# Routing phase: the root chain of a later round's norm on VectorE is woven between the ranking and the one-hot rows of this round

## What is computed

```python
h = _layernorm(x, axis=-1) * (1 + cb) + sb
X = h.reshape(-1, D)                       # 8192 tokens, D = 128
scores = sigmoid(X @ gate_w.T)             # E = 32 experts
_, idx = top_k(scores + bias, K)           # K = 4
w = take_along_axis(scores, idx, axis=-1)
w = w / clip(sum(w, axis=-1), 1e-12)
eid = idx.reshape(-1)
onehot = (eid[:, None] == arange(E)[None, :])
pos = take_along_axis(cumsum(onehot, axis=0) - 1, eid[:, None], axis=1)[:, 0]
valid = pos < C                            # C = 128 places per expert
...
xe = zeros((E, C, D)).at[eid, posc].add(where(valid[:, None], Xrep, 0))
```

## Time and profile before

| | us |
|---|---|
| median of 3 runs (lowest, highest) | 2204.21 (2203.22, 2204.34) |
| the profiled execution's own time | 2207.98 |
| its span, first to last instruction | 2206.2 |
| mean granted TensorE clock over the span | 0.869 of full |
| routing: DVE's first transpose of variances starts | 645.30 |
| routing: the last product `unit` (round 7) starts | 777.48 |
| routing: DVE's last instruction starts | 822.18 |

### The profile page before, as it was taken

How to read it: one execution, slowest core, us unless ns; L and a number is a source line. 1 busy time by engine, 2 the same in 40 slices (tenths; PEclk the granted TensorE clock), 3 DMA queues, 4 the chain that set the end, 5 groups by cost and what they waited for, 6 DMA issues and landing times. The chain is left out here.

```text
span 2206.2 us, 44205 instructions
## 1 busy us (share of the span) xinstructions
PE 1723.8 (78%) x13783; PEld 1360.8 (62%) x13783; DVE 1614.0 (73%) x4636; ACT 1338.3 (61%) x3234; POOL 1164.1 (53%) x1240
## 2 busy tenths in 40 slices
PE   5589999999956749569985777777777642999994
PEld 5478888888733434246653555555556532999993
DVE  7689999999948863369877999999655442555554
ACT  4468777777736882157764888887344331555551
POOL 3178777777710007722324888888525454444440
PEclk8699999999977658879987999999766555999997
DMA  3000000000040102341100000000311012222218
GB/s 114 14 2 2 2 2 2 2 2 2 2 182 31 41 30 47 39 133 58 48 1 1 1 1 1 1 1 1 155 34 35 32 40 62 68 66 65 65 50 233
DMA packets 103365, 92.10 MB, mean 42 GB/s; under 512 B 11696, under 2 KB 93616, under 8 KB 102432
## 3 DMA queue, kind: packets, MB, share of 16 engines
q1 hardware_dynamic: 80128, 62.84, 9.3%
q0 software_dynamic: 14560, 22.24, 3.8%
q10 hardware_dynamic: 8448, 4.20, 0.6%
HBM read 46.32 MB, written 42.91 MB: 40 GB/s over the span
## 5 line engine op out<-in xcount | busy, mean ns | idle before, releaser
L2253 POOL TENSOR_TENSOR delta_A<-delta_A,delta_sW 128x256 f32<-128x256 f32 x256 | 193.9, 758 | 79.5 <-ACT delta_sW L2100 53.5
L2023 PE MATMUL delta_u<-delta_m,tables_sb 128*128 128x256 f32 x512 | 166.7, 407 | 82.3 <-DVE delta_m L2173 82.3
L2873 POOL DMA_INDIRECT choice_rows<-ffn_y,ffn_xg x135 | 129.8, 962 | 169.9 <-DVE ffn_y L2980 164.7
L645 ACT ACTIVATE attn_p_att<-attn_score,attn_mx 128x224 f32<-128x224 f32 (+7 forms) x512 | 146.1, 397 | 107.2 <-DVE attn_mx L735 107.2
L630 ACT ACTIVATE attn_p_geo<-attn_kp_wide,attn_geo_cols 128x32 f32<-128x32 f32 (+6 forms) x448 | 179.5, 503 | 0.0
L2100 ACT ACTIVATE delta_sW<-delta_W,tables_sb 128x256 f32<-128x256 f32 x256 | 126.7, 506 | 80.5 <-DVE delta_W L2195 76.7
L573 PE MATMUL attn_score<-attn_k,attn_q_diag 128*128 128x64 f32 (+5 forms) x1024 | 175.4, 314 | 0.0
L2023 PEld LDWEIGHTS delta_u<-delta_m,tables_sb 128*128 128x128 f32 x512 | 87.3, 190 | 133.1 <-DVE delta_m L2173 126.3
L2019 PE MATMUL delta_u<-delta_v_own,tables_sb 128*128 128x256 f32 x512 | 154.1, 383 | 8.7 <-DVE xnT L2160 8.7
L587 PE MATMUL attn_out<-attn_turned,attn_v_diag 64*64 64x256 f32 (+7 forms) x4096 | 142.4, 288 | 14.6 <-DVE attn_turned L756 12.0
L2830 POOL DMA_INDIRECT rows<-mix_rows,mix_slot x128 | 124.3, 971 | 55.6 <-issue 51.5
(11 more groups left out here) (399 smaller groups left out, 4938.4 us busy)
## 6 DMA issues: line engine op xcount, KB each, us to landing
ffn_xg<-rows SPq DMA_DIRECT2D x135, 66.0 KB
acc<-route_zero SPq DMA_DIRECT2D x10, 832.0 KB
comb_rows<-choice_rows SPq DMA_DIRECT2D x32, 256.0 KB
rows<-route_rows SPq DMA_DIRECT2D x8, 640.0 KB, 3.4
load_rows<-in_x SPq DMA_DIRECT2D x16, 256.0 KB, 4.3
bT<-acc SPq DMA_DIRECT2D x16, 256.0 KB, 4.1
qT<-acc SPq DMA_DIRECT2D x16, 256.0 KB, 4.9
x_kept<-xT SPq DMA_DIRECT2D x16, 256.0 KB, 2.1
```

The costliest lines, as they stand in the source:

```text
L645: last = nc.scalar.activation(p_att[:, gr, PAIR_OFF[n]:PAIR_OFF[n] + SLOT * (n + 1)], score[at][:, c:c + SLOT * (n + 1)], ACT.Exp, bias=mx ...
L2023: nc.tensor.matmul(corrections(h, pp % 2), g.t("same_head"), m1[:, h].rearrange("p t d b -> p (t d b)"), start=False, stop=True).then_inc( ...
L2253: nc.gpsimd.tensor_tensor(A[:, t % 8], A[:, (t - 1) % 8], sW[:, t % RING], ALU.add).then_inc(k.A, 1)
L2873: nc.gpsimd.indirect_dma_start(g.choice_rows, bass.IndirectOffsetOnAxis(xg[:, n % RING, D:D + 1].bitcast(U32), 0), y[:, n % RING, :], None ...
```

## The change

In rounds 0 to 5, DVE no longer runs `norm(i + 2)` and then `rank(i)`. A new function `rank_beside_norm(i)` first places round i (`place`, `base`), and then issues the steps of the norm of round m = i + 2 alternately with the remaining steps of the ranking: the transpose of the variances, `own`, the add of epsilon, `slot`, the guess, the first one-hot row, and then each of the seven root steps followed by one more row. `spread_norm(m)`, the second transpose and the product `unit`, comes last. `rank` is split into `rank`, `own_places`, `own_slots` and `slot_row`. Each one-hot row now adds one to `by_slot_rest`, so its readers wait for 8 per round instead of 1. Rounds 6 and 7 and the norms of rounds 0 and 1 keep their order. Nothing is computed differently.

```diff
             def add_slots(i):
                 pe.wait_ge(c.by_slot, i + 1)
-                pe.wait_ge(c.by_slot_rest, i + 1)
+                pe.wait_ge(c.by_slot_rest, (CHOICES - BY_ACT) * (i + 1))
...
                 refine_roots(nc, dve, root_y[:, :], root_t[:, :], root_v[:, :], c.newton, ROOT * i)
+                spread_norm(i)
+
+            def spread_norm(i):
                 dve.wait_ge(c.newton, ROOT * (i + 1))
...
                 nc.vector.tensor_tensor(base[:, :], base[:, :], counts[:, SIDE * E0:WIDTH], ALU.add).then_inc(c.counted, 1)
+
+            def own_places(i):
+                dve.wait_ge(c.placed, i + 1)
                 nc.vector.tensor_tensor(own[:, :, :, :], onehots(i), place[:, :, None, :].to_broadcast([128, SIDE, K0, E0]),
                                         ALU.mult).then_inc(c.owned, 1)
+
+            def own_slots(i):
                 dve.wait_ge(c.owned, i + 1)
                 dve.wait_ge(c.counted, i + 1)
                 if i > 0:
                     dve.wait_ge(c.off, PARTS * i)
-                    dve.wait_ge(c.by_slot_rest, i)
+                    dve.wait_ge(c.by_slot_rest, (CHOICES - BY_ACT) * i)
                 nc.vector.tensor_reduce(slot[:, :], own[:, :, :, :].rearrange("p j c e -> p (j c) e"), AX.X, ALU.add).then_inc(c.slot, 1)
+
+            def slot_row(i, n):
                 dve.wait_ge(c.slot, i + 1)
                 if i > 0:
                     dve.wait_ge(c.slots_added, i)
-                for n in range(BY_ACT, CHOICES):
-                    last = nc.vector.tensor_scalar(by_slot[:, n, :], iota[:, :], slot[:, n:n + 1], None, ALU.is_equal)
-                last.then_inc(c.by_slot_rest, 1)
+                nc.vector.tensor_scalar(by_slot[:, n, :], iota[:, :], slot[:, n:n + 1], None, ALU.is_equal).then_inc(c.by_slot_rest, 1)
+
+            def rank_beside_norm(i):
+                m = i + 2
+                y, t, v = root_y[:, :], root_t[:, :], root_v[:, :]
+                step = ROOT * m
+                rank(i)
+                dve.wait_ge(c.var, m + 1)
+                nc.vector.transpose(turned_var[:, :, :].rearrange("p n i -> p (n i)"), var[:, :]).then_inc(c.var_turned, 1)
+                own_places(i)
+                dve.wait_ge(c.var_turned, m + 1)
+                nc.vector.tensor_scalar(v, turned_var[:, :, 0], LN_EPS, None, ALU.add).then_inc(c.v, 1)
+                own_slots(i)
+                dve.wait_ge(c.v, m + 1)
+                dve.wait_ge(c.inv, m)
+                nc.vector.tensor_scalar(y.bitcast(mybir.dt.int32), v.bitcast(mybir.dt.int32),
+                                        -0.5, Rstd.MAGIC, ALU.mult, ALU.add).then_inc(c.guess, 1)
+                slot_row(i, BY_ACT)
+                dve.wait_ge(c.guess, m + 1)
+                dve.wait_ge(c.newton, step)
+                nc.vector.scalar_tensor_tensor(t, y, Rstd.CUBE, y, ALU.mult, ALU.mult).then_inc(c.newton, 1)
+                slot_row(i, BY_ACT + 1)
+                dve.wait_ge(c.newton, step + 1)
+                nc.vector.tensor_tensor(t, t, v, ALU.mult).then_inc(c.newton, 1)
+                slot_row(i, BY_ACT + 2)
...
+                dve.wait_ge(c.newton, step + 6)
+                nc.vector.scalar_tensor_tensor(y, t, 1.5, y, ALU.add, ALU.mult).then_inc(c.newton, 1)
+                slot_row(i, BY_ACT + 7)
+                spread_norm(m)
 
             norm(0)
             norm(1)
             for i in range(0, LAST + 1):
                 choose(i)
                 if i + 2 <= LAST:
-                    norm(i + 2)
-                rank(i)
+                    rank_beside_norm(i)
+                else:
+                    rank(i)
+                    own_places(i)
+                    own_slots(i)
+                    for n in range(BY_ACT, CHOICES):
+                        slot_row(i, n)
```

More of the change, by code:

```diff
@@ L1239, in rank @@
                     dve.wait_ge(c.slots_added, i)
-                for n in range(BY_ACT, CHOICES):
-                    last = nc.vector.tensor_scalar(by_slot[:, n, :], iota[:, :], slot[:, n:n + 1], None, ALU.is_equal)
-                last.then_inc(c.by_slot_rest, 1)
+                nc.vector.tensor_scalar(by_slot[:, n, :], iota[:, :], slot[:, n:n + 1], None, ALU.is_equal).then_inc(c.by_slot_rest, 1)
[22 more added lines that the diff above has]
+                slot_row(i, BY_ACT + 2)
+                dve.wait_ge(c.newton, step + 2)
+                nc.vector.scalar_tensor_tensor(t, t, -1.25 / Rstd.CUBE, t, ALU.add, ALU.mult).then_inc(c.newton, 1)
+                slot_row(i, BY_ACT + 3)
+                dve.wait_ge(c.newton, step + 3)
+                nc.vector.scalar_tensor_tensor(y, t, 1.875, y, ALU.add, ALU.mult).then_inc(c.newton, 1)
+                slot_row(i, BY_ACT + 4)
+                dve.wait_ge(c.newton, step + 4)
+                nc.vector.scalar_tensor_tensor(t, y, -0.5, y, ALU.mult, ALU.mult).then_inc(c.newton, 1)
+                slot_row(i, BY_ACT + 5)
+                dve.wait_ge(c.newton, step + 5)
+                nc.vector.tensor_tensor(t, t, v, ALU.mult).then_inc(c.newton, 1)
+                slot_row(i, BY_ACT + 6)
+                dve.wait_ge(c.newton, step + 6)
+                nc.vector.scalar_tensor_tensor(y, t, 1.5, y, ALU.add, ALU.mult).then_inc(c.newton, 1)
+                slot_row(i, BY_ACT + 7)
+                spread_norm(m)
```

## The result

| | before | after |
|---|---|---|
| median, us (lowest, highest) | 2204.28 (2203.22, 2207.67) | 2238.05 (2230.82, 2241.76) |
| ratio to before, 95% interval | | 1.0147 [1.0128, 1.0166] |
| profiled execution, us | 2207.98 | 2230.82 |
| its span, us | 2206.2 | 2229.0 |
| routing, first transpose of variances to DVE's last instruction, us | 645.30 to 822.36: 177.1 | 645.19 to 852.27: 207.1 |

What follows compares the result with a forecast made beforehand. No engine bounds the whole; in routing, a loop through DVE, ACT and PE holds the round. The first round's 3.5 us plus 22.2 for five rounds make 25.7, put on 2204.21: 2229.9 us, range 2217 to 2242.

Steps and rivals of the forecast that it cites:

- The loop: In routing's steady rounds: variances, `unit`, scores, `route_rows`, next variances hold the round, 18.89 us in one, mean 18.58.
- the wait for the counts: On DVE, `place` must wait for PE's counts, queued behind the variances: 1.20 us added per round.
- DVE's smaller work: DVE's own work shrinks by 1.45 us per round, costed at nothing since DVE does not hold the round.
- its busy time would change little: Sign in the new profile: DVE's busy time in the routing phase changes little, as durations overlap.
- `place` to `unit`: DVE's new woven order from `place` to the product `unit` takes 7.5 us, against 4.58 on the loop before.
- `unit` to scores: From the start of DVE's product `unit` to ACT's scores, kept at 7.27 us per round.
- rival (b): PE's clock, with PE idle longer: scores 8.35 us after `unit` in all rounds, 5.4 us more, 2235.3 us; chance 0.13.
- Behind the last product: After the last product in routing nothing changes: ACT's order is the same, and scores of round 7 wait as before.
- The one-hot rows and `slots_added`: First row, at 10.41 us after `route_rows`, nearly meets the end of PE's `slots_added` work at 10.48: 0.1 us, left out.
- (a): On DVE, alternating root steps and rows do not overlap: `place` to `unit` 9.9 us, total 2244.5 us; chance 0.08.
- (c): PE at 2.4 GHz makes scores and variances faster: 12.5 us less over five rounds, 2217.4 us; chance 0.10.
- (d): DVE itself holds the round, so its 1.45 us less counts six times: 8.7 us, 2195.5 us; chance 0.03.

Runs made afterwards that it cites:

- experiment 3: Changed kernel with the transpose of the variances moved ahead of `place`: 2224.91 us, ratio 1.0112 to the kernel before.
- Experiment 4: Changed kernel with 60 added matmuls of zeros per round on PE while it waits for `unit`: 2220.02 us, ratio 1.0079 to the kernel before.
- experiment 2: Kernel before with the whole `rank(i)` ahead of `norm(i + 2)`, nothing woven: 2245.13 us, ratio 1.0201 to the kernel before.
- 10: Changed kernel with `count(i)` ahead of `variance(i + 2)` on PE: 2181.08 us, ratio 1.0109 to the kernel before.
- (6): Kernel before with `copy_rows` three one-hot rows earlier on ACT: 2156.24 us, ratio 0.9996 to the kernel before.
- Experiment 9: The changed kernel measured once more, in the third set of runs: 2187.32 us, ratio 1.0141 to the kernel before.
- experiment 5: Kernel before with added matmuls of zeros where PE waits: 2150.38 us, ratio 0.9972; repeated, 2150.32 us, ratio 0.9968.
- experiment 11: Kernel before with PE kept busy by matmuls of zeros and one-hot rows woven into `choose(i + 1)`: 2146.68 us, ratio 0.9955.

## Why the prediction was right, and by how much it was off

**The forecast and the time.** The direction was right and the length of a round nearly so (23.0 us forecast, 23.65 measured), but 2238.05 us lies outside the case that was given 0.63, 2226 to 2234, and inside the range because that took in the low clock.

**The loop.** Right. It was read as variances, `unit`, scores, `route_rows`, variances, and in the changed kernel every experiment that shortened or lengthened a piece of it moved the time the right way: the transpose put into the wait (3), PE's pieces made faster (4), 1.47 us added (2), the wait for the counts taken away (10, though the wait for `slots_added` took most of it back). In the kernel before, `copy_rows` moved earlier (6) did not show in the time. DVE's smaller work bought nothing, as costed; that its busy time would change little was wrong, it fell by 5.2 us in the five rounds.

**The wait for the counts**, forecast 1.20 us: measured 1.20.

**`place` to `unit`**, forecast 7.5 us: measured 7.49 in five of the six rounds and 7.85 in one (below). The distances of the old timeline, for instructions that need each other and for those that don't, could be added as they stood. The rule that the prediction quoted from the Trainium skill, page "VectorE: DVE Perf Modes", section "The DRAIN you can't avoid", would have had 9.9 here; the trace does not agree with it for instructions that are independent. The same section goes on to say that "A next op that is not held starts earlier", and with that the trace agrees, so the page contradicts the weaving less than the prediction had it. (The advice to save instructions stands in that page's section "Rules for kernel authors".)

**`unit` to scores**, forecast 7.27 us: this is the term that was mis-sized. It took 6.86, 8.35, 8.35, 7.30 and 8.36 us, mean 7.84, so 0.57 more in each of five rounds, 2.9 us (the old mean was 7.16). It was the prediction's rival (b), and it came true in three rounds of five. PE sat idle 4.9 to 8.9 us ahead of `center` instead of 0.4 to 1.6 in four rounds and 5.4 in one. It ran the centred values of all five rounds at the low clock (granted 0.50, 3.78 us), where one of five had the high one before, and the logits of three rounds wholly so (3.46 us), where that was one before. Experiment 4, which fills the idle stretch, brings both to the high clock. Idle time ahead of `center` is not the whole of it, though: the 8.35 us round of before had 0.55 us there, and experiment 3 with 4.7 to 8.3 us had no such round.

**Behind the last product**, forecast 0: scores of round 7 came 7.04 us after `unit` instead of 6.13, 0.9 us, with PE's logits at a granted clock of 0.50 instead of 0.70.

**The sum.** Forecast 3.5 + 22.2 = 25.7. Measured from the products: the first 3.64 us late, the five rounds 118.24 - 92.88 = 25.4, and 0.9 behind: 29.9; the phase began 0.11 us earlier, which makes its 30.0. Of the 3.2 us by which the five rounds exceed 22.2, `unit` to scores is 2.9 and the one late `unit` 0.36. Experiment 9 has the same 30 us on its whole time as well. The first measurement's 33.8 leaves 4 that I cannot place; 30 lies within its interval, 25.7 does not.

**The one-hot rows and `slots_added`**, forecast 0.1 us and left out: it showed in one of the five rounds, the one whose `add_slots` ran at the low clock (granted 0.50, 2.74 us instead of the 1.53 of the other four). It ended 10.48 us after `route_rows`, the very figure of the prediction, the first row started 0.18 us late, and `unit` 0.36, with a second small gap behind that row for which the trace names no cause. Experiments 2, 3 and 10 show how thin the margin was.

**Rivals.** (a), no overlap, is refuted by the rows of the new trace and by experiment 2. (c), PE at 2.4 GHz, is what experiment 4 makes by force: 2220.02 us, with before at 2201.34 in that set, which is 3 us lower than where the prediction stood; it was put at 2217.4. (d), DVE as the bound, is not true of the changed kernel, where DVE idles 7.8 us a round. It is true of the old order in experiment 5 and in the trace of 6, and the most that was ever gained there is a few us.

## What to carry to other kernels

A chain of small dependent instructions has gaps, and independent work put into them costs that engine less (1.47 us less for one norm and ranking, experiment 2); but it is the moment of the chain's last product that others wait for, and weaving two pieces of work makes both end when the later ends. So first ask who waits for each piece, and put no long steps ahead of a product that two engines stand waiting for. Weaving what nobody waits for (experiment 11) did no harm that can be told, and took work from DVE, but time is won by it only where that engine sets the round. And when a loop gets longer, look at what a longer idle stretch does to PE's clock, and at the semaphores that were met with a tenth of a microsecond to spare.

## What had not been expected of the hardware

Matmuls of zeros that do no work made a kernel faster: 60 per round in five rounds, 4.2 us of PE time each where PE stood idle, took 13.7 us off the phase. And the length of the phase repeats between two traces of the changed kernel to 0.1 us, round by round (22.6, 24.1, 24.1, 23.4, 24.1 us), granted clock included, while the whole kernels differ by 44 us: the first matmul of the delta phase stands at 1219.7 and 1221.7, one of its last at 1592.1 and 1593.7, and the first of the ffn phase at 1888.0 and 1842.4. Nearly all of the difference lies between the last two, in the mix phase, which writes its rows to memory by indirect transfers. What makes it long or short was not tried.
